# Cross-attention and mixture-of-experts block: two of ScalarE's four v copies ahead of the exp, and TensorE's mask ahead of the output projection

## The reference

```python
S, D, H, HD, E, F = 64, 128, 16, 8, 8, 512        # 128 batches
xn = layernorm(x)
q, k, v = xn @ Wq.T, ctx @ Wk.T, ctx @ Wv.T       # split into 16 heads
scores = where(causal, (q @ k.T) * HD ** -0.5, -1e9)
x = x + (softmax(scores) @ v) @ Wo.T
z = layernorm(x)
rw = softmax(z.mean(over the tokens) @ Wr + br)   # two experts a batch
h = gelu(z @ W1[e] + b1[e])
y = z + sum over the two of weight * (h @ W2[e] + b2[e])
out = x + layernorm(y) * gamma + beta
```

## Time and profile before

| what | us |
|---|---|
| median of 3 runs | 616.57 (615.7 to 618.05) |
| the profiled execution: time / span | 616.13 / 614.2 |
| busy in the span: PE, DVE, ACT, POOL | 548.9, 524.4, 496.2, 453.7 |
| exp L596, probsT copy L607 (128 each) | 80.0, 76.4 |
| v copies L540 (128 of 271 ns) | 34.7 |
| mask L343 (256 of 273 ns) | 69.9 |

### The profile page before, as it was taken

One profiled execution on the slowest core, in us unless ns is written; L12 is line 12 of the kernel. 1 busy time (PEld: TensorE's weight loads), 2 busy tenths in 40 slices (PEclk: granted clock), 3 DMA queues, 4 the chain that ended last, 5 costly groups with the idle time before them and its releaser, 6 DMA issues.

```text
span 614.2 us, 18949 instructions
## 1 busy us (share of the span) xinstructions
PE 548.9 (89%) x4481; PEld 384.0 (63%) x4481; DVE 524.4 (85%) x1473; ACT 496.2 (81%) x1156; POOL 453.7 (74%) x783
## 2 busy tenths in 40 slices
PE   3899999999999999999998617999999999999883
PEld 2556565555555655656555314888788878878672
DVE  3899999999999999999998566888888898898677
ACT  3788888888888888888888627888888888888494
POOL 6789999999999999999997644656555665554355
PEclk9999999999999999999999957999999999999887
DMA  4010101010101000100020011123312331322135
GB/s 121 28 36 11 36 26 34 9 34 26 34 9 34 26 18 25 34 9 15 11 77 2 2 34 56 53 67 91 91 58 62 99 95 56 93 63 65 44 104 171
DMA packets 55568, 30.03 MB, mean 49 GB/s; under 512 B 4840, under 2 KB 54512, under 8 KB 55536
## 3 DMA queue, kind: packets, MB, share of 16 engines
q1 hardware_dynamic: 55104, 29.47, 16.4%
q10 hardware_dynamic: 432, 0.20, 0.1%
HBM read 13.00 MB, written 4.19 MB: 28 GB/s over the span
## 4 chain that ended last, share of the span: by engine, by line
PE 66%; DVE 14%; issue 11%; ACT 5%; DVEq 2%; ACTq 1%; POOL 1%; DMA 0%; POOLq 0%
PE scores_banks L354 9%; PE bank_pair L365 6%; PE scores_banks L484 5%; PE bank_pair L497 5%; PE scores_banks L486 5%; PE scores_banks L485 5%; PE bank_pair L498 5%; PE bank_pair L499 5%; PE bank_pair L378 5%; PE bank L390 5%; ACT v_blocks L540 3%; PE scores_banks L343 3%; DVE scores_shifted L798 2%; PE bank L328 2%; DVE gelu L968 2%
## 5 line engine op out<-in xcount | busy, mean ns | idle before, releaser
L1086 POOL TENSOR_TENSOR probs<-probs,row_sum_recip 128x512 f32<-128x512 f32 x128 | 133.4, 1043 | 20.0 <-DVE row_sum_recip L804 15.0
L693 ACT ACTIVATE gelu<-scores_banks,b_expert 128x512 f32<-128x512 f32 x144 | 98.2, 688 | 26.5 <-PE scores_banks L486 20.5
L1135 POOL CAST gathered<-z_hi_lo (+1 forms) x114 | 45.2, 431 | 88.8 <-PE scores_banks L486 78.8
L788 DVE TENSOR_REDUCE row_max<-scores_banks 128x8 f32<-128x512 f32 x128 | 87.0, 679 | 18.6 <-PE scores_banks L354 18.4
L607 ACT ACTIVATE probsT<-bank_pair 128x512 f32<-128x512 f32 x128 | 76.4, 597 | 27.1 <-PE bank_pair L365 26.2
L596 ACT ACTIVATE probs<-scores_shifted 128x512 f32<-128x512 f32 x128 | 80.0, 625 | 19.3 <-DVE scores_shifted L798 15.7
L917 DVE SCALAR_TENSOR_TENSOR zT_then_yT<-bank_pair,slot_weight,zT_then_yT x288 | 74.3, 282 | 17.3 <-issue 15.6
L791 DVE TENSOR_REDUCE row_sum<-probs 128x8 f32<-128x512 f32 x128 | 86.8, 678 | 1.2 <-ACT probs L596 0.5
L798 DVE TENSOR_TENSOR scores_shifted<-scores_banks,row_max 128x512 f32<-128x512 f32 x128 | 86.6, 677 | 0.0
L354 PE MATMUL scores_banks<-k_by_head,qT 32*64 32x256 f32 x1024 | 84.8, 401 | 0.1
L365 PE MATMUL bank_pair<-ident,probs 128*128 128x128 f32 x512 | 83.9, 286 | 0.3 <-POOL probs L1086 0.2
(11 more groups left out here) (168 smaller groups left out, 1166.2 us busy)
## 6 DMA issues: line engine op xcount, KB each, us to landing
gathered<-z_hi_lo SPq DMA_DIRECT2D x187, 64.0 KB, 1.8
ctxT_pair<-in_ctxT SPq DMA_DIRECT2D x32, 128.0 KB, 2.1
w_raw<-in_w SPq DMA_DIRECT2D x16, 256.0 KB, 3.1
out<-gelu SPq DMA_DIRECT2D x16, 256.0 KB, 2.3
x_res<-in_x SPq DMA_DIRECT2D x14, 256.0 KB, 2.7
x_res<-in_x SPq DMA_DIRECT2D x1, 512.0 KB, 5.3
gathered<-z_hi_lo ACTq DMA_DIRECT2D x3, 64.0 KB, 1.9
wq<-in_wq SPq DMA_DIRECT2D x1, 64.0 KB, 2.5
```

What stands on the lines that cost most here:

```text
L693: nc.scalar.activation(G[:, c, :], bank[c][:, :], ACT.Gelu, bias=b1e).then_inc(a_g if c == 0 else a_gp, 1)
L788: nc.vector.reduce_max(mx, ps, AX.X).then_inc(v_max, 1)
L1086: nc.gpsimd.tensor_tensor(pp, pp, RC[:, k % 2, :].unsqueeze(2).to_broadcast([128, 8, S]), ALU.mult).then_inc(g_norm, 1)
```

## The change

On ACT the four v copies of a block are split. `prep_v` gets an argument j2: the copies to the lower 64 partitions of v_blocks (j2 = 0), with both waits, are issued ahead of the exp of step s = 0, the others (j2 = 1) behind it, where all four stood. On PE, at s = 0 alone, the mask for the next step is issued behind `prep_xk` and ahead of `project`; at s = 1 to 3 it stays last. Nothing is added or taken away: the same instructions, in another order on two engines.

```diff
@@ PE, steps
                     if s == 0 and more:
                         pe.wait_ge(d_ct[(h + 1) % 2], 16 * i + 16 * (h + 1))
                         prep_xk(P + 1, (h + 1) % 2)
+                    if s == 0 and (not static or U + 1 < NB):
+                        mask(i, u + 1)
                     if s == 0 and (not static or 0 <= P - 2 < NP):
                         project(4 * i + (2 * h - 3), 1, P - 3, P + 1 if not static else min(P + 1, NP))
...
-                    if not static or U + 1 < NB:
+                    if s > 0 and (not static or U + 1 < NB):
                         mask(i, u + 1)
@@ ACT, prep_v
-            def prep_v(P, par):
-
-                act.wait_ge(p_v, P + 1)
-                ge(act, p_pv, 4 * P - 4)
-                for j2 in range(2):
-                    for odd in range(2):
-                        ins = nc.scalar.activation(
...
+            def prep_v(P, par, j2):
+
+                if j2 == 0:
+                    act.wait_ge(p_v, P + 1)
+                    ge(act, p_pv, 4 * P - 4)
+                for odd in range(2):
+                    ins = nc.scalar.activation(
...
+                    ins.then_inc(a_v if j2 + odd == 2 else a_vh, 1)
@@ ACT, steps
+                    if s == 0 and (not static or 1 <= P < NP):
+                        prep_v(P, h, 0)
                     if not static or 0 <= U - 1 < NB:
                         act.wait_ge(v_sub, U)
                         ge(act, p_t, U - 4)
                         nc.scalar.activation(PP[:, (u - 1) % 4, :], SS[:, (u - 1) % 2, :], ACT.Exp,
                                              scale=SCALE).then_inc(a_exp, 1)
                     if s == 0 and (not static or 1 <= P < NP):
-                        prep_v(P, h)
+                        prep_v(P, h, 1)
...
-            prep_v(0, 0)
+            prep_v(0, 0, 0)
+            prep_v(0, 0, 1)
```

More of the change, by code:

```diff
@@ L533, in _ @@
         def _(act):
-            def prep_v(P, par):
-                act.wait_ge(p_v, P + 1)
-                ge(act, p_pv, 4 * P - 4)
-                for j2 in range(2):
-                    for odd in range(2):
-                        ins = nc.scalar.activation(
[L541 to L544, removed]
+            def prep_v(P, par, j2):
[4 more added lines that the diff above has]
+                    ins = nc.scalar.activation(
+                        VM[64 * j2:64 * j2 + 64, par, :, :, j2, :].rearrange("p (t o) g d -> p o t g d", o=2)[:, odd],
+                        J1[64 * odd:64 * odd + 64, 0:256].rearrange("p (t j g d) -> p j t g d", t=2, j=2, d=HD)[:, j2],
+                        ACT.Copy)
+                    ins.then_inc(a_v if j2 + odd == 2 else a_vh, 1)
             def prep_xk(P):
```

## The result

The changed kernel takes 601.9 us in the median of 4 runs (599.79 to 602.57), the kernel before 616.46 in the median of its 4 by then: ratio 0.9754, 95% interval 0.9735 to 0.9773. Forecast: 603.7, range 598.5 to 611.5. Timed once more beside the experiments it had 0.9755 (0.973 to 0.978).

The account below looks back on a forecast made before the run. All engines were nearly full in 10.39 us blocks, with PE stalled on the v copies. 27 x 0.45 = 12.2 plus 0.7 gives 12.9 off 616.13: 603.2, plus 0.44 for the median: 603.7 us, range 598.5 to 611.5.

Parts of the forecast that it names:

- the ring of ACT and PE through `prep_q`: Chain of waits from `prep_q` through ACT's copies back to PE's next `prep_q`; claimed longest after the change, 9.94 us a block.
- The two copies ahead of the exp fit its idle: On ACT at s = 0: two copies take 0.58 us, making the exp only 0.20 or 0.12 late.
- Release and arrival meet at the projection: At s = 0, PE arrives at 209.63 and ACT releases the bank for 209.65, so the projection's stall is gone.
- The price of the late exp: On DVE: the exp's 0.12 to 0.20 us adds to its 9.82 ring only if DVE is ahead of ACT.
- DVE's own: Chain of waits through DVE and the exp, row_max to next row_max: mean 9.82 us a block.
- C: Rival, chance 0.17: exp about 0.35 us late, DVE's ring becomes 10.17, half the gain comes back; 610.6 us.
- D: Rival, chance 0.05: the whole 0.58 us goes into DVE's ring, 10.40 a block, no gain; 616.6 us.
- What is late next: Which ring limits the attention block after the edit: ACT and PE's at 9.94 us, leaving 0.45 of 0.68 gained.
- The mask's 0.21: On PE at s = 0: the mask ahead of the projection brings the next scores 0.21 us closer behind it.
- The start and the end: Two blocks ahead of the 27 and one behind: half a block's gain each, 0.7 us, an estimate.
- POOL's floor of 9.80: POOL's own round of normalisations takes 9.80 us a block, the floor below which blocks would not fall.
- B: Rival, chance 0.20: PE isn't held at `prep_q`, that ring shrinks to 9.54 and POOL's 9.80 decides; 600.0 us.

Follow-up runs that it names:

- four ahead: As the changed kernel, but all four v copies stand ahead of the exp at s = 0; 614.49 us, ratio 0.9955 to the kernel before.
- x and k first: As the changed kernel, but at s = 1 ACT copies x and k ahead of the exp instead of behind it; 599.5 us, ratio 0.9716.

## Why the prediction was right

The time (603.7 against 601.9), the sign and the mechanism held: the stall at the projection went, the ring of ACT and PE through `prep_q` took its place. Two of its terms were wrong by more than they show in the sum.

- *The two copies ahead of the exp fit its idle.* Right in sum, not in parts. From the start of z's high half to the third copy I had 0.32 + 0.58 + 0.53 = 1.43; it is 200.84 - 199.43 = 1.41. But the exp starts 0.47 behind the pair's first copy instead of 0.58, and the next copy 0.64 behind the exp instead of 0.53. The two misses of 0.11 cancel, and that is luck. The 0.38 that the prediction gives two copies with an overlap is 0.35 by its own figures (twice 0.27, less twice 0.09); its sum does not use it.
- *Release and arrival meet at the projection.* Right: the copies end at 201.41, the projection starts at 201.55, the mask 0.23 ahead of it. No wait is left to see, but it still restarts, 0.68 long: the scores come 0.61 behind it instead of the 0.54 of an unstalled one, which the kernel with four ahead does show (k projection to projection 0.65, scores 0.54 behind).
- *The price of the late exp.* Nothing, as the sum had it, but not for its reasons. The exp was to be 0.20 and 0.12 late; it is 0.04 and 0.00 later behind DVE's shifted scores than before. With four copies ahead it is 0.65 and 0.57 later, and the block 10.33; but the ring that makes it is the one through the residual, `turn_z`, PE and ACT, where the prediction (rivals C and D) would have put DVE's own. Two copies fit the idle, four do not; that is the reason for splitting them at all.
- *What is late next.* Right: the ring of ACT and PE through `prep_q`. An extra copy in it costs its full 0.19 and a copy beside it nothing. I had 9.94, it is 9.87 to 9.88: `prep_q` starts 0.06 behind the copy of x and k, where I had taken the 0.14 of the projection, and 0.02 lies in the copies. That is 0.07 x 27 = 1.9 us, as large as the difference between 603.7 and 601.9; the runs themselves spread over 2.8 us, so it can't be told closer.
- *The mask's 0.21.* The scores do follow 0.22 sooner, but the term's worth in the total is 0.09 to 0.10, since `prep_q` takes back the rest. The prediction had this in its ring; my expectation for the mask alone forgot it, and missed. The ring that the mask shortens on top of the split is that of the copies and the projection, 9.97, and `prep_q`'s 9.87 stops it.
- *The start and the end.* 0.7 was an estimate. The 27 blocks gave 27 x 0.518 = 14.0 of the 14.9 us, 0.9 lay outside them.
- *POOL's floor of 9.80* is at most 9.77, since blocks of 9.77 were reached. *The granted clock* stayed 1.00.

The rivals: C (610.6) would have needed the exp 0.35 late, and it is 0.04 late at most. B needed PE free at `prep_q`; x and k first gave that and the block went to 9.82. With z's high half moved too, hiding POOL's waits changed nothing, so there POOL is not the limit. Rings of 9.77 to 9.88 lie so close that each move past the changed kernel bought 0.1 or less: x and k first is the best of the versions run, 0.9716 (0.9698-0.9735) against 0.9755, and its interval still touches the changed kernel's.

## What to carry to other kernels

When all engines are busy nine tenths of a loop's time, add up each ring of waits (through two or three engines, back to the same instruction one block later) from the starts of neighbouring rows, and take the longest one that is left after the edit: here that forecast 0.45 a block where the edited place alone promised 0.7. Work can be moved ahead of an instruction that waits, up to its idle time; what goes beyond arrives at whoever needs that instruction, here at `turn_z`, two engines on. A forecast that hits does not show that its ring was the right one: look in the profile for the wait or the stretched record that closes it. A stall that is shorter than a matmul shows in no list of waits, only as a longer matmul pair and a late successor.

## What the runs showed of the hardware

- ACT overlaps neighbours unevenly. An exp follows a 64x128 copy 0.10 before that copy's end, a copy behind the exp of s = 0 starts 0.53 behind the exp's start in the kernel before and 0.64 in the changed one, with the same two operations and no wait listed; the copies among themselves stand 0.29 apart at 0.27 each. Why the 0.53 became 0.64 stays open. What differs is that these copies write the upper 64 partitions of v_blocks, but a copy of the probabilities directly behind an exp stands just as far off (0.66 with four copies ahead, 0.63 with x and k first), so that alone does not explain it.
- A TensorE pair whose input comes at the last moment shows 0.10 more duration (0.70 against 0.60) and 0.10 more to its successor (0.53 against 0.43). With the copies split alone, a wait of 0.24 ahead of the projection is in no list either.
- The stage behind the attention, the same in all these kernels, varied from 259.8 to 261.5 us between executions (without the two that sum z there).
